# Softmax graph layers on one Trainium2 core: scores of the next unit moved behind the contexts, and VectorE's maximum behind all four context tiles

## The reference

```python
x = _layernorm(x + _L0_gnn_ref(x, adj, ...), axis=-1)   # two gated layers
x = _layernorm(x + _L1_gnn_ref(x, adj, ...), axis=-1)   # two softmax layers
```

```python
u = jnp.einsum('bid,bjd->bij', h, h) / temper
a = jax.nn.softmax(u, axis=-1)
delta = a * adjacency_matrix
attn = delta / (jnp.sum(delta, axis=-1, keepdims=True) + 1e-10)
hl, hs, hr = h @ wl.T + b_l, h @ ws.T + b_s, h @ wr.T + b_r
ctx = (attn * upper) @ hl + diag_a[..., None] * hs + (attn * lower) @ hr
o = (ctx - mean) / jnp.sqrt(var + LN_EPS) * g + beta;  h = relu(o)
```

## Time and profile before

| | us |
|---|---|
| median of 3 runs | 1929.68 |
| lowest, highest | 1921.40, 1932.85 |
| profiled execution, first to last instruction (span) | 1928.1 |
| softmax phase, of the span | 878 to 1928 |
| PE busy, of the span | 1800.2 (93%) |
| DVE busy | 1467.2 (76%) |
| ACT busy | 917.9 (48%) |
| POOL busy | 783.4 (41%) |

### The profile page before, as it was taken

One profiled execution on the slowest core, in us unless ns is written; L12 is line 12 of the kernel. 1 busy time (PEld: TensorE's weight loads), 2 busy tenths in 40 slices (PEclk: granted clock), 3 DMA queues, 4 the chain that ended last, 5 costly groups with the idle time before them and its releaser, 6 DMA issues.

```text
span 1928.1 us, 31714 instructions
## 1 busy us (share of the span) xinstructions
PE 1800.2 (93%) x10208; PEld 1663.0 (86%) x10208; DVE 1467.2 (76%) x3023; ACT 917.9 (48%) x1834; POOL 783.4 (41%) x769
## 2 busy tenths in 40 slices
PE   7999999999999999987999998989999989899994
PEld 6989898888889898876988988979889889798894
DVE  4586867768685958686787797887887977978978
ACT  4546454545555464643534444445345444444442
POOL 4142423323342423243444363453443544525434
PEclk9999999999999999998998998989989989999997
DMA  6004020203011020213002002002011020020100
GB/s 205 7 23 139 27 82 13 96 5 103 5 63 46 22 87 22 82 35 119 1 18 71 19 19 82 3 19 82 3 59 45 19 82 3 19 82 3 68 1 33
DMA packets 76412, 92.25 MB, mean 48 GB/s; under 512 B 29621, under 2 KB 67509, under 8 KB 76345
## 3 DMA queue, kind: packets, MB, share of 16 engines
q1 hardware_dynamic: 76344, 91.53, 14.4%
HBM read 53.76 MB, written 25.17 MB: 41 GB/s over the span
## 4 chain that ended last, share of the span: by engine, by line
PE 29%; DVE 16%; issue 6%; ACT 2%; DVEq 0%; POOL 0%; ACTq 0%; POOLq 0%
PE s_work L1113 17%; PE s_work L1125 5%; PE b_score_ps L114 3%; DVE s_prob_lo L1392 3%; DVE b_ht L1342 3%; DVE s_v_full L1371 1%; DVE s_prob L1383 1%; DVE b_z L1410 1%; DVE s_expo L1380 1%; PE b_score_ps L116 1%; PE b_turn L1079 1%; DVE b_z L1437 1%; PE b_score_ps L109 1%; PE b_score_ps L1100 1%; ACT b_z L1220 1%
## 5 line engine op out<-in xcount | busy, mean ns | idle before, releaser
L1113 PE MATMUL s_work<-b_w_hi,b_ht 128*128 128x384 f32 x2304 | 636.5, 346 | 64.4 <-DVE s_v_full L1371 47.5
L1113 PEld LDWEIGHTS s_work<-b_w_hi,b_ht 128*128 128x128 f32 x2304 | 427.2, 191 | 80.5 <-DVE s_v_full L1371 53.9
L1113 PE MATMUL s_work<-b_w_lo,b_ht 128*128 128x384 f32 x1152 | 391.6, 340 | 0.0
L380 PE MATMUL g_work<-b_ht,b_w_hi 128*128 128x512 f32 x1152 | 357.7, 392 | 10.3 <-DVE b_w_lo L706 10.3
L1273 POOL TENSOR_TENSOR s_v_lo<-s_v_full,s_v_hi 128x384 fp32r<-128x384 f32 x256 | 266.5, 1057 | 228.7 <-ACT s_v_hi L1206 227.9
L641 POOL TENSOR_TENSOR g_qv_lo<-g_v_full,g_qv_hi 128x384 fp32r<-128x384 f32 x128 | 132.9, 1057 | 376.4 <-ACT g_qv_hi L520 376.4
L380 PEld LDWEIGHTS g_work<-b_ht,b_w_hi 128*128 128x128 f32 x1152 | 216.5, 189 | 51.9 <-issue 10.3
L1206 ACT ACTIVATE s_v_hi<-s_v_full 128x384 fp32r<-128x384 f32 x256 | 125.6, 520 | 250.1 <-DVE s_v_full L1371 250.0
L380 PE MATMUL g_work<-b_ht,b_w_lo 128*128 128x512 f32 x576 | 225.8, 392 | 0.0
L1113 PEld LDWEIGHTS s_work<-b_w_lo,b_ht 128*128 128x128 f32 x1152 | 220.3, 191 | 0.0
L729 DVE TENSOR_TENSOR g_qv_lo<-g_work,g_qv_hi 128x512 fp32r<-128x512 f32 x192 | 128.8, 688 | 118.3 <-ACT g_qv_hi L508 116.5
(11 more groups left out here) (148 smaller groups left out, 3697.3 us busy)
## 6 DMA issues: line engine op xcount, KB each, us to landing
b_x_in<-in_x_t SPq DMA_DIRECT2D x16, 768.0 KB, 7.0
g_x_res<-in_x SPq DMA_DIRECT2D x16, 768.0 KB, 7.8
b_x_in<-x SPq DMA_DIRECT2D x16, 768.0 KB, 5.0
s_x_res<-b_x_in SPq DMA_DIRECT2D x16, 768.0 KB, 6.4
x<-b_z SPq DMA_DIRECT2D x15, 768.0 KB, 3.8
out<-b_z SPq DMA_DIRECT2D x15, 768.0 KB, 3.8
b_a_tr<-in_adj_t SPq DMA_DIRECT2D x64, 64.0 KB, 2.4
g_a_nat<-in_adj SPq DMA_DIRECT2D x32, 64.0 KB, 2.4
```

Source lines behind the costliest of these rows:

```text
L380: mm = pe.matmul(bank[:], w, h, start=(n == 0), stop=(n == len(pairs) - 1))
L1113: mm = pe.matmul(bank[:, 0:H], h, w, start=(n == 0), stop=(n == len(pairs) - 1))
```

## The change

TensorE issues the contexts of a unit first and the scores of the next unit behind them. VectorE takes all four context tiles, then the offset of the final norm where there is one, and then the next maximum.

```diff
                     for j in range(9, VB):
                         values(i, unit, j)
+                    contexts(i, unit)
                     if more:
                         scores(i, unit + 1)
-                    contexts(i, unit)
...
                 dve.wait_ge(sums_ready, nth(i, unit, 1, 0))
-                contexts_out(i, unit, (0,))
+                contexts_out(i, unit, range(NT))
+                if s is not None:
+                    final_offset(i, s)
                 if more:
                     maximum(i, unit + 1)
-                    if s is not None:
-                        final_offset(i, s)
-                contexts_out(i, unit, range(1, NT))
-                if s is not None and not more:
-                    final_offset(i, s)
```

## The result

| | before | changed |
|---|---|---|
| median of the runs, us | 1928.83 (4 runs) | 1953.05 (4 runs) |
| lowest, highest | 1921.40, 1932.85 | 1949.06, 1956.19 |
| span of the profiled execution | 1928.1 | 1954.4 |

The ratio is 1.0128 (95% interval 1.0098 to 1.0157): the change costs 24 us, 1.3%. Predicted were 1955.5 us, with 1938 to 1983 as the range.

What follows compares the result with a forecast made beforehand. TensorE's stalls or slower clock were taken to bound the softmax phase. The terms 12.8 + 23.1 + 5.3 - 7.2 - 8.2 gave +25.8 us, so 1955.5 us, with a range of 1938 to 1983.

Steps and rivals of the forecast that it cites:

- Part 1, the wait for the maximum: In 17 light units TensorE stands 0.75 us at the transpose of the maxima, waiting for the maximum: +12.8 us.
- Part 2, heavy units with the clock up: In seven heavy units contexts 1 and 3 wait for banks; maximum wait included, +3.3 us each, +23.1 us.
- Part 2, the clock: In seven heavy units already at 1.2 GHz the reordering costs nothing, only the 0.75 us maximum wait: +5.3 us.
- rival 1: Clock falls in all 14 heavy units and runs into the scores, 1.7 us each: +24 us, 1979 us; chance 0.21.
- Part 3a, the loop turn: VectorE's loop turn behind unit 0 begins earlier, shortening TensorE's waits in unit 1: 1.2 us in six turns, -7.2 us.
- Part 3b, VectorE's lead: In heavy units earlier second joins shorten the stall before the last value by 0.27 or 1.0 us: -8.2 us.
- Rival 3: Earlier joins in heavy units gain nothing, small shifts lengthening as many instructions as they shorten: 1964 us; chance 0.12.

## Why the prediction was right

The time came to within 2.5 us of it, but two terms were off in opposite directions, the clock by +10 us and the loop turn by -7, and nearly cancel. That the total is so close is luck; that it lies in the range is not, since either error alone would have stayed in it.

**Part 1, the wait for the maximum**: 0.75 us said, 0.70 measured in ten light units, and 0.52 us idle before the transpose, where 0.6 was said. Right. The copy, the join and the maximum follow as the rows of before had them.

**Part 2, heavy units with the clock up**: banks 9 and 11 are what contexts 1 and 3 wait for, and the one of bank 11 ends last (shown by the kernels with these additions moved). Unit 3 went from 32.3 to 35.8 us where the clock stays up; with the 0.63 us that the stall at value 1 cost in the next unit, +2.9 against 3.3 - 0.27 said. Right.

**Part 2, the clock**: this is the term that was mis-sized. I left it as it was, slow behind unit 0's stall and nowhere else, and named a change of its pattern as a sign of being wrong; that sign came. The clock left the long stretches behind unit 0's stall for the most part (37.5 to 35.85 us), and fell instead behind the later waits in six of the 14 units, four of unit 3 (38.3 to 38.5 us three times, 37.4 once) and two of unit 0 (38.6 and 39.2). That is rival 1's mechanism: a fall that begins at the later waits runs into the scores, some 2.5 us a time. In sum the heavy units cost +30 us from transpose to transpose, where the prediction has 23.1 + 5.3 - 8.2 = 20. So of rival 1's 24 us 10 came.

The Trainium skill (TensorE: Matmul & The Clock Gate, "HAM oscillation") has repeated pauses bring the slower clock each time. The traces agree in one kernel: with biases 9 and 10 early, a pause of 3.5 to 5.0 us in each heavy unit had a fall to 1.2 GHz behind it every time. In the changed kernel, with pauses of 1.8 us or less before the contexts, the clock fell behind one of them in six units of 14. The pauses in the page's example are longer than those that rival 1 counted on, so the page spoke for that rival less than the prediction says.

**Part 3a, the loop turn**: said -7.2 us beside six times the 0.75, which makes -2.7 from transpose to transpose; measured -9.5. I had counted one wait and a little of the next. The turn took 3.0 us instead of 4.1, against my doubt that it might take longer, and the waits for transposes and features went entirely: the units behind the turn had been 2.3 us longer than other light ones (31.15 against 28.8), and are 0.1 to 0.4 us longer now. That the pause is the instruction fetch was not tried; the profile says only "issue".

**Part 3b, VectorE's lead**: the stalls went from 2.65 and 3.35 to 2.2 and 2.25, where 2.4 and 2.4 were said. The joins came at 4.0 us, not 4.2. Rival 3, that lateness has nothing to do with it, is out. I took the start of the second join after the start of value 1, and the stall before value 11, from the traces of the kernel before, the changed one and the seven kernels up to the one with the scores between the contexts. In the 126 heavy units of these nine that have a unit behind them, unit 3 and unit 0 alike:

```
second join, us after value 1     4.0-4.1     4.4     4.6-4.7     5.4-5.5     5.7
number of heavy units             50          14      26          5           31
stall before value 11, us         2.2-2.3     2.5-2.6 2.6-2.7     3.3-3.4     3.3-3.4
```

The stall goes with lateness in all of them, whatever the order of the engines. But it is no straight line of 0.64 us per us: it rises by about 0.8 up to 5.4 and then stays. GpSimd's collisions are the link by the durations, but no run took GpSimd's work away, so that is argued. On the rule of the Trainium skill (SBUF — State Buffer, "Who interferes with whom") the residual additions agree: they have two SBUF inputs, and four take 3.44 instead of 1.96 us beside GpSimd's split. What rival 3 made of the rule, that a small shift lengthens as many instructions as it shortens, did not hold.

## What to carry to other kernels

Before two pieces of work on the busiest engine change places, look at what each of them covers: here the scores covered the wait for two banks, the contexts covered the way to the maximum, and the swap uncovered both; putting the scores behind the first context alone covers both again. A wait that another wait stands behind costs nothing. Taking it away gains nothing, and here it cost 53 us: what moved met GpSimd, the wait left over became 3.5 to 5.0 us long, and TensorE's slower clock came behind it in every heavy unit. The best gain stood ahead of all this, in one short instruction that freed a bank late because it was queued behind work that nobody waited for as urgently.

## What was not expected of the hardware

Where the clock falls decides what it costs. In a unit such as that of 1392.61 above it falls at the stall before value 11 and only shortens the wait before context 1 (0.41 for 1.7 us). Behind context 3 it runs into the scores: with a wait of 3.5 us or more the mean granted clock from 916 to 1820 us is 0.93, and each of the 14 heavy units loses 2.8 to 3.8 us behind it. With two waits around 2.1 us of matmuls it is 0.96, and six of 14 lose up to 3.3 us. Whether the length of the pause or its being one piece makes the difference is not shown, since both changed together; one piece of 1.56 us, at 1532.00, had a fall behind it too.

The pause of VectorE at its loop turn is not of one length either. From the start of the last instruction before it to the next it is 4.1 to 4.2 us where that was a statistics instruction (4.9 in the first turn), and 3.0 to 3.3 us where it was the last of the maximum. That holds for the seven kernels of either kind. Of it 3.5 to 3.7 (4.3 in the first turn) and 2.8 to 3.2 us are idle. Why is open.
